# A machine loop of five iterations written out as straight code, its gates turned into plain waits, and the first group's start reordered

## The reference, cut to what matters

```python
x = x + tanh(g_xattn[0]) * performer(layernorm(x), ctx, ctx, features)   # layer 0 attention
x = x + tanh(g_ffn[0])   * rwkv_ffn(layernorm(x), W_r, W_k, W_v, mu_r, mu_k)
x = x + tanh(g_xattn[1]) * gated_attention(ctx, layernorm(x), w_kv, w_q, w_la, w_proj, b_proj, att_weight)
x = x + tanh(g_ffn[1])   * bitlinear_ffn(layernorm(x), w_gate, w_up, w_down)
# performer: k_kernel = exp(h_k + proj_k - max(h_k)), the max over all keys of all sequences
# gated_attention: a = softmax(q k); a2 = softmax(gate * a); (w * a2 + (1 - w) * a) @ v
```

## Time and profile before

| | us |
|---|---|
| runs of the kernel before, median of 3 | 559.25 |
| lowest and highest of them | 555.53, 562.09 |
| the profiled execution, its own time | 562.33 |
| span of that execution, first to last instruction | 560.6 |
| TensorE busy | 453.3 (81% of the span) |
| VectorE busy | 416.8 (74%) |
| ScalarE busy | 372.7 (66%) |
| GpSimd busy | 300.9 (54%) |
| mean granted TensorE clock over the span | 0.948 of full |

### The profile page before, as it was taken

How to read it: one execution, slowest core, us unless ns; L and a number is a source line. 1 busy time by engine, 2 the same in 40 slices (tenths; PEclk the granted TensorE clock), 3 DMA queues, 4 the chain that set the end, 5 groups by cost and what they waited for, 6 DMA issues and landing times.

```text
span 560.6 us, 19430 instructions
## 1 busy us (share of the span) xinstructions
PE 453.3 (81%) x7511; PEld 343.8 (61%) x7540; DVE 416.8 (74%) x1372; ACT 372.7 (66%) x769; POOL 300.9 (54%) x415
## 2 busy tenths in 40 slices
PE   0467589999999999799969997999969998867632
PEld 0255457676767677577757674877667776655521
DVE  3522367698989898689859887789868989897734
ACT  1523655678787878578767877587857878675532
POOL 4322045576667575466637574657546666563610
PEclk9999999999999999899979999899989999998765
DMA  7501010100101010201010101001010100000000
GB/s 174 127 2 36 4 33 8 35 8 2 49 4 48 5 48 4 50 3 46 6 46 8 41 10 33 20 2 49 6 46 4 46 5 19 5 19 8 6 10 11
DMA packets 35110, 15.21 MB, mean 27 GB/s; under 512 B 12497, under 2 KB 34897, under 8 KB 35025
## 3 DMA queue, kind: packets, MB, share of 16 engines
q1 hardware_dynamic: 32528, 12.79, 9.2%
q10 hardware_dynamic: 2496, 1.14, 0.8%
HBM read 9.73 MB, written 2.10 MB: 21 GB/s over the span
## 4 chain that ended last, share of the span: by engine, by line
PE 60%; ACT 11%; DVE 10%; issue 10%; POOL 5%; DMA 1%; ACTq 0%; POOLq 0%; DVEq 0%
PE TP L1447 10%; PE MC L1480 9%; PE FP L1355 7%; PE MA L1371 6%; PE FP L1334 4%; PE SP L1438 3%; ACT ft L611 3%; PE FP L1338 2%; PE FP L1336 2%; PE SP L1551 2%; ACT ft L612 2%; ACT E L648 2%; DVE WT L958 2%; PE FP L1297 2%; POOL ft L402 2%
## 5 line engine op out<-in xcount | busy, mean ns | idle before, releaser
L1480 PEld LDWEIGHTS MC<-Vc,ET 128*64 128x64 f32 x2048 | 68.7, 143 | 43.5 <-issue 43.5
L1480 PE MATMUL MC<-Vc,ET 128*64 128x25 f32 x2048 | 75.0, 222 | 19.1 <-issue 15.2
L402 POOL TENSOR_SCALAR ft<-ft 128x512 f32<-128x512 f32 x64 | 39.5, 617 | 74.9 <-ACT ft L612 71.4
L425 POOL TENSOR_TENSOR Zn<-E,rsh 128x1024 f32<-128x1024 f32 x32 | 60.9, 1902 | 22.6 <-DVE rsh L1018 21.3
L433 POOL TENSOR_TENSOR Zn<-Zn,Gs 128x1024 f32<-128x1024 f32 x32 | 60.9, 1902 | 3.2 <-DVE Gs L1029 1.7
L958 DVE TENSOR_TENSOR WT<-FP,mask 128x512 f32<-128x512 f32 x64 | 43.7, 684 | 24.2 <-PE FP L1355 24.1
L659 ACT ACTIVATE ET<-TP 128x512 f32<-128x512 f32 x64 | 37.9, 595 | 25.9 <-PE TP L1447 25.9
L1355 PE MATMUL FP<-ft 32*64 32x64 f32 x2048 | 41.7, 236 | 15.4 <-POOL ft L402 9.9
L1355 PEld LDWEIGHTS FP<-ft 32*64 32x64 f32 x2048 | 37.8, 148 | 24.3 <-issue 24.3
L653 ACT ACTIVATE ET<-TP 128x512 f32<-128x512 f32 x64 | 37.9, 596 | 11.1 <-PE TP L1447 10.2
L998 DVE TENSOR_REDUCE mx<-SP 128x16 f32<-128x1024 f32 x32 | 39.0, 1219 | 6.9 <-PE SP L1438 6.7
(11 more groups left out here) (195 smaller groups left out, 1167.3 us busy)
## 6 DMA issues: line engine op xcount, KB each, us to landing
Cd<-in_ctx SPq DMA_DIRECT2D x32, 128.0 KB, 2.8
kX<-kT SPq DMA_DIRECT2D x256, 8.0 KB
X<-in_x SPq DMA_DIRECT2D x16, 128.0 KB, 2.2
call<-in_ctx SPq DMA_DIRECT2D x4, 512.0 KB, 10.5
out_x<-X SPq DMA_DIRECT2D x16, 128.0 KB, 1.9
wffn<-in_L_ffn_w_gate ACTq DMA_DIRECT2D x1, 256.0 KB, 3.8
wffn<-in_L_ffn_w_up ACTq DMA_DIRECT2D x1, 256.0 KB, 4.3
wffn<-in_L_ffn_w_down ACTq DMA_DIRECT2D x1, 256.0 KB, 6.6
```

Source lines behind the costliest of these rows:

```text
L402: pool.tensor_scalar(f, f, EPS_K, 1.0, ALU.add, ALU.mult).then_inc(s("ftp"), 1)
L425: pool.tensor_tensor(z, E1[u][:, :].rearrange("p (h m) -> p h m", m=64), rsh[u][:, :].unsqueeze(2).to_broadcast([P, H, 64]), ALU.subtract) ...
L1480: last = mm(MC[64 * j:64 * j + 64, c + 32 * q:c + 32 * q + 25], weights[:, q, 64 * j:64 * j + 64], Vc[g.p][:, 2 * u + j, q, 0:25], start=T ...
```

## The change

Four edits. The loop is gone, and all 20 steps are written out on each engine; with that `g.k` is a plain integer in every step, and `at_ends` waits in all of them. `gate_at` is gone: each gate becomes a plain `at` with the same semaphore and value. On VectorE the `gmask`, `Rf` and `Nh` operations and their waits become a function `early()`, called in step 0 just before `nbA`, behind `stA` and `mvA`. On ScalarE the wait for the gains and the tangent move from the head of the program into `prepare()`, behind `yA`, the split of the values' weights, `squares_T` and `rows_T` of step 0 and ahead of the four squares of `ctx`; the wait for the tangent's own completion is dropped.

```diff
-    def gate_at(eng, s, value, passed):
-        if not isinstance(value, int) or value > 0:
-            eng.wait_ge(s, value)
-            eng.sem_inc(passed, 1)
...
-        LOOP = (6, NG)
-        START = list(range(LOOP[0]))
-        END = list(range(LOOP[1], NG + STAGES - 1))
+        STEPS = NG + STAGES - 1
         def run(eng, step, late=None):
-            for m in START:
+            for m in range(STEPS):
                 step(*place(m))
-                if m == START[1] and late:
+                if m == 1 and late:
                     late()
-            with eng.Fori(LOOP[0] // 2, LOOP[1] // 2) as i:
-                for q in range(2):
-                    step(*loop_place(i, q))
-            for m in END:
-                step(*place(m))
...
             def veA(g):
-                gate_at(pool, s("mvA"), g.k * 2 + 2, s("pool_passed"))
+                at(pool, s("mvA"), g.k * 2 + 2)
                 var_eps("A")
...
             act.wait_ge(s("cst"), CST)
-            act.wait_ge(s("g_in"), 48)
-            act.activation(tg[:, :], gains[:, 0:4], ACT.Tanh).then_inc(s("tg"), 1)
-            act.wait_ge(s("tg"), 1)
...
             def prepare():
+                act.wait_ge(s("g_in"), 48)
+                act.activation(tg[:, :], gains[:, 0:4], ACT.Tanh).then_inc(s("tg"), 1)
                 for c in range(4):
...
-            v.wait_ge(s("cst"), CST)
...
-            v.wait_ge(s("r_in"), 16)
...
-            v.wait_ge(s("cstv"), CSTV)
+            def early():
+                v.wait_ge(s("cst"), CST)
...
+                v.wait_ge(s("r_in"), 16)
...
+                v.wait_ge(s("cstv"), CSTV)
...
                 if a:
+                    if a.first:
+                        early()
                     nbA(a)
```

More of the change, by code:

```diff
@@ L219, in __init__ @@
                 self.k, self.p, self.half = k, p, half
-                self.first = isinstance(k, int) and k == 0
+                self.first = k == 0
         def group(k):
@@ L227, in place @@
             return [group(m - t) for t in range(STAGES)]
-        def loop_place(i, q):
-            return [Group(i * 2 + (q - t), (q - t) % 2, i + (q - t) // 2) for t in range(STAGES)]
         STAGES = 5
@@ L367, in veB @@
             def veB(g):
-                gate_at(pool, s("mvB"), g.k * 2 + 2, s("pool_passed"))
+                at(pool, s("mvB"), g.k * 2 + 2)
                 var_eps("B")
@@ L377, in veC @@
             def veC(g):
-                gate_at(pool, s("mvC"), g.k * 2 + 2, s("pool_passed"))
+                at(pool, s("mvC"), g.k * 2 + 2)
                 var_eps("C")
@@ L387, in veD @@
             def veD(g):
-                gate_at(pool, s("mvD"), g.k * 2 + 2, s("pool_passed"))
+                at(pool, s("mvD"), g.k * 2 + 2)
                 var_eps("D")
@@ L397, in ftp @@
             def ftp(g, w):
-                gate_at(pool, s("fe"), g.k * 4 + 2 + 2 * w, s("pool_passed"))
+                at(pool, s("fe"), g.k * 4 + 2 + 2 * w)
                 for t in range(2):
@@ L441, in quant_int @@
             def quant_int(g):
-                gate_at(pool, s("xm"), g.k * 2 + 2, s("pool_passed"))
+                at(pool, s("xm"), g.k * 2 + 2)
                 pool.tensor_scalar(xq[:, :, :], xm[:, :, :], -MAGIC, 1.0, ALU.add, ALU.mult).then_inc(s("xq"), 1)
             def ffn_round(g, u):
-                gate_at(pool, s("hmg"), g.k * 2 + 1 + u, s("pool_passed"))
+                at(pool, s("hmg"), g.k * 2 + 1 + u)
                 pool.tensor_scalar(hq[u][:, :], hmg[u][:, :], -MAGIC, 1.0, ALU.add, ALU.mult).then_inc(s("hq"), 1)
@@ L793, in _ @@
                 v.memset(Vb[64 * h:64 * h + 64, :, :, 16 * h + 8:16 * h + 9], 1.0).then_inc(s("cstv"), 1)
-            v.wait_ge(s("cst"), CST)
[L795 to L798, removed]
-            v.wait_ge(s("r_in"), 16)
[L800 to L805, removed]
-            v.wait_ge(s("cstv"), CSTV)
+            def early():
+                v.wait_ge(s("cst"), CST)
+                for b in range(4):
+                    r = slice(32 * b, 32 * b + H)
+                    v.tensor_scalar(gmask[r, H * (b // 2):H * (b // 2) + H], ident[r, 32 * b:32 * b + H], 0.5, None, ALU.mult)\
+                        .then_inc(s("setup"), 1)
+                v.wait_ge(s("r_in"), 16)
+                for g in range(4):
+                    v.scalar_tensor_tensor(Rf[:, g, :].rearrange("p (h m) -> p h m", m=MF),
+                                           blk[:, g, :].rearrange("p (h m) -> p h m", m=MF), S1,
+                                           rrep[:, :].unsqueeze(1).to_broadcast([P, 4, MF]), ALU.mult, ALU.mult)\
+                        .then_inc(s("setup"), 1)
+                v.tensor_scalar(Nh[:, :, :], blk[:, :, :], -0.5 * S2, None, ALU.mult).then_inc(s("setup"), 1)
+                v.wait_ge(s("cstv"), CSTV)
             def prepare():
@@ L879, in mvA @@
             def mvA(g):
-                gate_at(v, s("stA"), g.k * 2 + 2, s("dve_passed"))
+                at(v, s("stA"), g.k * 2 + 2)
                 aggr("A")
@@ L894, in mvB @@
             def mvB(g):
-                gate_at(v, s("stB"), g.k * 2 + 2, s("dve_passed"))
+                at(v, s("stB"), g.k * 2 + 2)
                 aggr("B")
@@ L909, in mvC @@
             def mvC(g):
-                gate_at(v, s("stC"), g.k * 2 + 2, s("dve_passed"))
+                at(v, s("stC"), g.k * 2 + 2)
                 aggr("C")
@@ L924, in mvD @@
             def mvD(g):
-                gate_at(v, s("stD"), g.k * 2 + 2, s("dve_passed"))
+                at(v, s("stD"), g.k * 2 + 2)
                 aggr("D")
@@ L1326, in features @@
                     at(pe, s("kT"), g.k)
-                    gate_at(pe, s("qcT"), g.k + 1, s("pe_passed"))
+                    at(pe, s("qcT"), g.k + 1)
                 elif w == 1:
@@ L1330, in features @@
                     at_ends(pe, g, s("kT"), g.k)
-                    gate_at(pe, s("fe"), g.k * 4 + 2, s("pe_passed"))
+                    at(pe, s("fe"), g.k * 4 + 2)
                 strips = [(32 * i, 512 * (i % 2), i) for i in (2 * w, 2 * w + 1)]
@@ L1346, in weights0 @@
                     at_ends(pe, g, s("WT"), g.k * 4)
-                    gate_at(pe, s("ftp"), g.k * 4 + 4, s("pe_passed"))
+                    at(pe, s("ftp"), g.k * 4 + 4)
                 elif u == 1:
-                    gate_at(pe, s("WT"), g.k * 4 + 2, s("pe_passed"))
+                    at(pe, s("WT"), g.k * 4 + 2)
                 for j in range(2):
@@ L1364, in out0 @@
                     at(pe, s("vals"), g.k * 2 + 2)
-                    gate_at(pe, s("gate"), g.k * 2, s("pe_passed"))
+                    at(pe, s("gate"), g.k * 2)
                 elif u == 1:
-                    gate_at(pe, s("WT"), g.k * 4 + 4, s("pe_passed"))
+                    at(pe, s("WT"), g.k * 4 + 4)
                 for q in range(8):
@@ L1432, in scores @@
                     at(pe, s("QT"), g.k + 1)
-                    gate_at(pe, s(f"kX{g.p}"), g.half * 256 + 256, s("pe_passed"))
+                    at(pe, s(f"kX{g.p}"), g.half * 256 + 256)
                 elif u == 1:
-                    gate_at(pe, s("ls"), g.k * 2 + 1, s("pe_passed"))
+                    at(pe, s("ls"), g.k * 2 + 1)
                 for hh in range(2):
@@ L1493, in outA @@
                     at(pe, s("n1"), g.k * 2 + 1)
-                gate_at(pe, s("F"), g.k * 4 + 2 + 2 * u, s("pe_passed"))
+                at(pe, s("F"), g.k * 4 + 2 + 2 * u)
                 out1(g, u, ET1[u], 0, "oA")
@@ L1504, in outB @@
                 at_ends(pe, g, s("out"), g.k * 2 - 2)
-                gate_at(pe, s("S"), g.k * 4 + 2 + 2 * u, s("pe_passed"))
+                at(pe, s("S"), g.k * 4 + 2 + 2 * u)
                 out1(g, u, ET2[u], 256, "oB")
```

## The result

The changed kernel takes 542.66 us (median of four runs, 540.78 to 546.79) where the kernel before, run beside it, takes 560.50 us. The ratio is 0.9707, with a 95% interval of 0.9616 to 0.9797: faster by 3%, 17.8 us. The forecast was 540.0 us within 534 to 546 us. The profiled execution is the slowest of the four, 546.79 us with a span of 545.0 us, against 562.33 and 560.6 us before.

What follows compares the result with a forecast made beforehand. TensorE was taken as the bound, stalling at each jump back. 562.33 - 18.2 (loop) - 3.0 (gates) + 0.8 (head) = 541.9 us, or 538.8 us less the profiled execution's excess; 540.0 us was chosen between, range 534 to 546 us.

Steps and rivals of the forecast that it cites:

- the likeliest case: Whole kernel: the forecast together with Rival 4, 534 to 545 us, chance 0.84.
- What bounds the kernel: Steady steps: TensorE is the bound with little slack; each jump back costs idle time and a slow stretch behind it.
- Part 1, the loop: Steps 5 to 16: written out, eleven periods take 306.0 us instead of 324.20 us, so 18.2 us go.
- each would now be a straight one: Steps 5 to 16: every period becomes that of a written-out step, 27.82 us, with `at_ends` waits included.
- Part 2, the gates: Gates on VectorE and GpSimd: 0.10 to 0.15 us saved each on the path, together 3 us, bounds 0 and 5.
- TensorE's gates stand behind other waits: TensorE's gates: the last wait stays its own instruction, so worth nothing, at worst 0.1 us each either way.
- Part 3, the head: Program start: `nbA` 0.6 us earlier, but table load and tangent join the path; net 0.8 us lost.
- then 1.23 us of `Rf` and `Nh` end at about 13.0 us: Head, VectorE: after `gmask`, these operations end there, so `nbA` starts at 13.05 us instead of 13.69.
- Rival 1: Ten middle steps: added waits are not hidden, 1.4 us a step, 14 us, giving 554 us; chance 0.08.
- Rivals 2 and 3: Instruction fetch: stalls only move, about 557 us (chance 0.05), or each block crossing stalls TensorE, 570 us (chance 0.03).
- Rival 4: Head and gates: table load hidden, gates at their upper bound, some 537 us; chance counted within the forecast's 0.84.

Runs made afterwards that it cites:

- e6: The kernel before with the machine loop over steps 6 to 11 only, two jumps back instead of four; 552.13 us, ratio 0.9892.
- e4: The kernel before with only the loop written out, its gates and head kept; 542.51 us, ratio 0.9734.
- e1: The changed kernel with the old head: VectorE's constants ahead of step 0, the tangent ahead of `yA`; 536.04 us, ratio 0.9588.
- e9: e1 with TensorE's ten `gate_at` lines back, those of GpSimd and VectorE still gone; 540.21 us, ratio 0.9686.
- e3: The changed kernel with one more wait: GpSimd starts its large clears only when VectorE's `Nh` is done; 537.01 us, ratio 0.9609.
- e7: e1 without the `at_ends` waits in steps 6 to 15, as the loop had left them out; 533.01 us, ratio 0.9589.

## Why the prediction was right, and where its steps failed

The forecast of 540.0 us missed the median by 2.7 us, within its range, and the likeliest case is the one that came. Its sum held by luck: two terms were wrong in opposite directions, the gates by 3.5 us and the head by 3.6 us at `yA`.

1. **What bounds the kernel** was right: TensorE's steps, with a stall at each jump. Half the jumps gave about half the gain (e6, 9.8 of 17.5 us in the profiles).
2. **Part 1, the loop,** forecast at -18.2 us, is -17.5 us in the profile of e4 over the twelve periods and -19.1 us in its runs. The step "each would now be a straight one", 27.82 us, measured 27.88 us in e4.
3. **Part 2, the gates,** forecast at -3.0 us with bounds 0 and 5, is -6.5 us (e4 against e1), outside its bounds. The step that failed is "TensorE's gates stand behind other waits [...]; I count them at nothing". They cost 0.21 us a step in the profiles (e9). The rows to see it were at hand: in the kernel before `weights0` starts 0.25 us behind `ftp` in step 5, where the gate has other waits ahead of it, and 0.14 us in step 7, where it is alone. For the gates that it did count the prediction was near: 0.10 to 0.15 us each forecast, 0.1 us before `ftp` measured, and 2.3 us from e9 to e4, across two sets, where it had 3.0 us.
4. **Part 3, the head,** forecast at +0.8 us with bounds -0.5 and +1.0, is +4.4 us at `yA` against the kernel before. Against e1, which has the old head and the same early loads, it is +5.5 us at `yA`, and +5.9 to +6.6 us in the runs (541.94 and 542.66 us against 536.04 us; they include what step 2 adds). The step that failed is "then 1.23 us of `Rf` and `Nh` end at about 13.0 us": a duration was carried from a stretch in which GpSimd was idle into one in which it clears its large buffers. GpSimd's `prepare()` follows `rsA` directly, and the edit pulled `rsA` ahead of `Nh`. Mended by one wait (e3), the head costs 1.0 us against e1, near the forecast. The rest of the part held: the table load between `nbA` and `yA`, the tangent's 0.2 us, and the second half of `Cd`, which landed at 9.3 us where 10.2 us was forecast, early like all the loads.
5. **Rival 1,** the added waits, was priced at 14 us if none were hidden and put at 0.25 us a step by the rows; they measure 0.35 us a step (e7), 3.0 us in all by the runs. The bound of 27 a step was low, too: e7 has 32 a step less than e1. They were inside the straight period that the sum used, so the sum was safe; that they could be dropped was missed.
6. **Rivals 2 and 3** fall: in the changed kernel no period from step 4 to 16 is longer than 27.68 us, so no block of the instruction stream stalls the array. **Rival 4**'s hidden table load did not come.

## What to carry to other kernels

Before moving an operation, look at what the other engines will be doing at its new time: a duration is a property of the place too, above all between VectorE and GpSimd. A wait costs latency mainly where its engine is starved, and there every wait instruction ahead of the deciding one counts, so redundant waits belong out of a written-out steady state. When one chain is shortened, list the loads that join it further on; those bound the gain.

## What the runs showed of the hardware

TensorE's jump back in the machine loop took 3.3 to 4.9 us in the branch instruction, while the other engines' took at most 0.067 us. The kernel with four jumps scatters over 9 us (554.8 to 564.1 us in one set of runs) and e1 over 1 us, but two other kernels without jumps scatter too (e4 over 7.7 us, e7 over 6.4 us), so the jumps are not the only cause. One VectorE operation on 128x512 float32 waited through four consecutive GpSimd clears, 5.29 us in place of 0.42 us: the block did not end with the clear that was running. At `weights0` TensorE starts 0.04 us behind the releaser where a plain wait is alone (e7), 0.14 us where other waits stand ahead of it (e1) or where it is alone and followed by a count-up (step 7 of the kernel before), and 0.25 us with both (e9, e4). The share of the granted clock read 1.00 from 70 to 85 us in the changed kernel while its matmuls took 1.7 times as long as later (1.98 against 1.16 us).
